# Order of the correlation, the weighted adds and the transpositions in a software-pipelined FFT-attention, mixing and LoRA-expert kernel

## What is computed

```python
# 1. LoRA of the sample's adapter, then autocorrelation attention over it
Bx = einsum('bni,bri->bnr', x, B[id]);  y = einsum('bnr,bor->bno', Bx, A[id])
corr = irfft(rfft(y) * conj(rfft(y)))             # per row, length 1024
weights, delay = top_k(corr, 6)                   # log(1024) -> 6
x = x + sum_k softmax(weights)_k * roll(y, -delay_k)
# 2. the sample's 64x64 channel mixing, then a dense layer with LoRA experts (top 2 of 8)
z = einsum('bct,bcd->bdt', x, W[id2])
x = x + z @ W_base.T + b_base + lora_experts(z)
```

## Time and profile before

| what | value |
|---|---|
| median of 3 runs | 948.55 us (946.2 to 956.33) |
| profiled execution, first to last instruction (span) | 948.1 us |
| mean granted TensorE clock, core 0 | 0.956 |
| busy: TensorE / its weight loads / VectorE / ScalarE / GpSimd | 839.0 / 705.7 / 620.8 / 336.3 / 478.5 us |

### The profile page before, as it was taken

How to read it: one execution, slowest core, us unless ns; L and a number is a source line. 1 busy time by engine, 2 the same in 40 slices (tenths; PEclk the granted TensorE clock), 3 DMA queues, 4 the chain that set the end, 5 groups by cost and what they waited for, 6 DMA issues and landing times. The chain is left out here.

```text
span 948.1 us, 16004 instructions
## 1 busy us (share of the span) xinstructions
PE 839.0 (88%) x4808; PEld 705.7 (74%) x4808; DVE 620.8 (65%) x1362; ACT 336.3 (35%) x617; POOL 478.5 (50%) x465
## 2 busy tenths in 40 slices
PE   4646899998998998998988989989989989999978
PEld 3645788777777787777877877777867778778766
DVE  2245667867677676766677576766667766777772
ACT  5343334233433333333442334333333333333311
POOL 1244544746575552755556355655337544555530
PEclk9856999999999999999999999999999989999998
DMA  8466576676766776665767667667666667777441
GB/s 277 140 195 203 185 232 213 211 239 197 232 201 203 237 240 185 212 217 184 234 202 242 192 195 214 194 208 226 193 209 194 206 212 223 234 235 234 166 146 45
DMA packets 66796, 194.48 MB, mean 205 GB/s; under 512 B 13708, under 2 KB 24236, under 8 KB 63540
## 3 DMA queue, kind: packets, MB, share of 16 engines
q0 software_dynamic: 23040, 83.90, 28.1%
q1 hardware_dynamic: 32084, 71.33, 26.8%
q10 hardware_dynamic: 11616, 38.67, 10.4%
HBM read 118.36 MB, written 50.33 MB: 178 GB/s over the span
## 5 line engine op out<-in xcount | busy, mean ns | idle before, releaser
L1093 POOL DMA_INDIRECT rolled<-y_d,off x160 | 168.6, 1054 | 297.9 <-DVE row L939 191.0
L939 DVE SCALAR_TENSOR_TENSOR row<-rolled,weight,row 128x1024 f32<-128x1024 f32 x160 | 226.5, 1416 | 101.7 <-DMA rolled<-y_d,off 98.6
L463 PE MATMUL o_ps<-wt_hi,x_hi 128*128 128x512 f32 x512 | 219.6, 429 | 0.0
L463 PE MATMUL o_ps<-wt_hi,x_lo 128*128 128x512 f32 x512 | 202.2, 395 | 0.0
L463 PE MATMUL o_ps<-wt_lo,x_hi 128*128 128x512 f32 x512 | 201.7, 394 | 0.0
L1082 POOL TENSOR_TENSOR row<-row,bias 128x1024 f32<-128x1024 f32 x32 | 77.7, 2427 | 88.1 <-PE x_ps L570 88.1
L570 PE MATMUL x_ps<-mix,row 128*128 128x128 f32 x512 | 76.5, 311 | 50.5 <-DVE row L939 32.6
L570 PEld LDWEIGHTS x_ps<-mix,row 128*128 128x128 f32 x512 | 70.4, 220 | 63.4 <-DVE row L939 38.2
L463 PEld LDWEIGHTS o_ps<-wt_hi,x_hi 128*128 128x128 f32 x512 | 96.6, 189 | 22.5 <-issue 4.8
L463 PEld LDWEIGHTS o_ps<-wt_hi,x_lo 128*128 128x128 f32 x512 | 96.2, 188 | 22.1
L463 PEld LDWEIGHTS o_ps<-wt_lo,x_hi 128*128 128x128 f32 x512 | 97.0, 189 | 14.6
(11 more groups left out here) (130 smaller groups left out, 1485.5 us busy)
## 6 DMA issues: line engine op xcount, KB each, us to landing
y_d<-y ACTq DMA_DIRECT2D x64, 512.0 KB, 3.6
row<-in_x SPq DMA_DIRECT2D x32, 512.0 KB, 7.0
adapter<-g_hi SPq DMA_DIRECT2D x64, 256.0 KB, 4.5
out<-row SPq DMA_DIRECT2D x32, 512.0 KB, 2.9
adapter<-g_lo SPq DMA_DIRECT2D x32, 256.0 KB, 4.5
r<-in_L_cond_A SPq DMA_DIRECT2D x72, 64.0 KB
r<-in_L_cond_B SPq DMA_DIRECT2D x56, 64.0 KB, 2.0
rolled<-in_L_ffn_W_base SPq DMA_DIRECT2D x5, 512.0 KB, 6.0
```

What stands on the lines that cost most here:

```text
L463: last = pe.matmul(dst, a, b, start=start and n == 0, stop=stop and n == len(todo) - 1)
L939: dve.scalar_tensor_tensor(row[u][:, :], rolled[n % RB][:, :], weight[:, n:n + 1], row[u][:, :], ALU.mult, ALU.add).then_inc(sum_step, 1)
L1093: pool.indirect_dma_start(out=rolled[n % RB][:, :], out_offset=None, in_=y2_d[u], in_offset=bass.IndirectOffsetOnAxis(ap=off[:, n:n + 1], ...
```

## The change

Three moves; no instruction is added or taken away.

1. On TensorE both halves of `x_transposed(s)` stand at the head of the slot, ahead of `project(t)`, and no longer behind the steps c = 0 and c = 1 of `base`.
2. On TensorE `correlation(s)` stands ahead of `mixed(s-1)` and no longer behind it.
3. On VectorE the low part `eo_lo` of tile s's powers stands ahead of the last weighted add (number 4) of tile s-1 and no longer behind it.

```diff
             def slot(s, u, i):
                 t, g = s - LAG, i + 1
                 attn, ffn, prep = has_attn(s), has(t), has_group(g)
+                if attn and not first(s):
+                    x_transposed(s, u, i, 0)
+                    x_transposed(s, u, i, 1)
                 if ffn:
                     project(t)
                 for c in range(KC):
                     if ffn:
                         base(t, c)
-                    if c < 2 and attn and not first(s):
-                        x_transposed(s, u, i, c)
...
                 if ffn:
                     experts(t)
+                if attn:
+                    correlation(s)
                 if has(s - 1):
...
                     mixed(s - 1, *before(u, i, 1))
-                if attn:
-                    correlation(s)
...
                 if has(last):
-                    for n in range(1, NSEL):
+                    for n in range(1, NSEL - 1):
...
                         add_rolled(last, ul, n)
                 if has_attn(s):
                     dve.wait_ge(eo_h, s + 1)
                     low(eo_lo[:, :, :].rearrange("p a r -> p (a r)"), eo[:, :, :].rearrange("p a r -> p (a r)"),
                         eo_hi[:, :, :].rearrange("p a r -> p (a r)")).then_inc(eo_l, 1)
+                if has(last):
+                    add_rolled(last, ul, NSEL - 1)
```

## The result

| | before | after |
|---|---|---|
| median | 950.45 us (4 runs, 946.2 to 956.33) | 1007.78 us (4 runs, 1006.98 to 1008.63) |
| ratio | | 1.0582, 95% interval 1.0536 to 1.0627 |
| profiled span | 948.1 us | 1006.8 us |
| mean granted TensorE clock | 0.956 | 0.921 |

The change makes the kernel 5.8% slower; predicted were 1009 us. The total is right, but several of its terms are not, as will be seen. Every ratio here is of executions in the usual state; the one of 4529.41 us that came up among ten of the kernel with move 1 alone isn't in its ratio.

What follows compares the result with a forecast made beforehand. The prediction took the chain through powers, `eo_lo`, correlation, `x_lo` and maximum, not TensorE's work, to bound the kernel. 948.1 + 52 + 8 = 1008 us of span, 1009 us as median; range 975 to 1036.

Steps and rivals of the forecast that it cites:

- What bounds the kernel: In the slot without group work, the chain of last gather, powers, `eo_lo`, correlation and maximum bounds, with the mixing hidden.
- 50 us or more: Sign in the profile after: the correlation's total wait for `eo_lo`, in nearly every slot, where 7.4 us stood.
- Correlation ahead of the mixing: At the slot's end on TensorE: mixing waits for correlation, `x_lo` ends 3.98 us after mixing starts; no early maximum.
- `eo_lo` ahead of the last add: On VectorE: the moved add, about 1.3 us, costs nothing beside the correlation; `eo` is ready 0.97 us earlier.
- 0.1 more for folds: In slots with u = 0: 0.1 us added for GpSimd's folds, within a total of +2.65 us.
- Both transpositions at the head: On TensorE at the slot's head, while the mixed tile is copied: cost 0 to 1.2 us, taken as 0.
- The 0.35 us: Per-slot gain from the earlier transposed x, bounds 0 and 0.5 us; add 0 waits for its gather and stays.
- The sum of the chain, +52 us: Slot without group work +2.2 us; six loop turns 39, slots 28 to 31 8.8, slots 1 to 3 about 4.5.
- The slots with group work: In the loop: u = 0 +2.65 us, u = 1 +0.3, u = 2 +1.1, u = 3 +2.3; a turn say 6.5.
- The clock, +8 us: Low TensorE clock behind the hole before the correlation: a third of 28 slots, 14 us, less about 6; bounds 0 and 42.
- Rival 1: Early results shorten the slot's first half more; loss about 1 us per slot, 979 us; chance 0.18.
- Rival 2: The low clock in every slot, as TensorE's hole recurs in each: 1036 us; chance 0.12.

Runs made afterwards that it cites:

- the filler: All three moves plus 14 unused transpositions on TensorE between experts and correlation, against the kernel before: 980.94 us, ratio 1.0293.
- the pieces earlier: Kernel before with move 1 and TensorE's product with B, small pieces, spectrum and adapter_out one step of base earlier: 966.18 us, ratio 1.0113.

## Why the prediction was right or wrong

- *What bounds the kernel.* Right: the powers' chain, not TensorE's work. The new wait is the one named, 68.1 us for `eo_lo` where "50 us or more" was said, and filling the waits brought nothing of the 57.9 us. Moves 2 and 3 alone each confirm that the order at the slot's end decides.
- *Correlation ahead of the mixing.* Right in mechanism: 3.88 us from the mixing's start to the end of `x_lo` (3.98 predicted), the correlation right behind `eo_lo`. The reason that I gave, that the maximum stands behind `x_lo`, is not the whole of it: with the maximum ahead of `x_lo` the kernel was slower still, because then `x_lo`, `base` and the product with B came some 3 us later.
- *`eo_lo` ahead of the last add.* Right for the moved add, which lies beside the correlation. The gain on GpSimd was 0.69 us and not 0.97, and not where I had it: the last power is short, but the one ahead of it is long. For u = 0 "0.1 more for folds" was near: the moved add was drawn out by 1.0 us, of which the mixing waits 0.24 with the filler. The rule of the Trainium skill, "SBUF — State Buffer", "Who interferes with whom", which I had cited against the change, named this place, and the trace agrees: the add of 2.29 us ends 1.08 us behind the fold that it lay beside.
- *Both transpositions at the head.* Right: 0 within the interval, alone and in company. The 0.35 us that I gave them for the slot's beginning was not theirs.
- *The sum of the chain, +52 us.* Too large. The term that failed in the plain slot is the 0.35 us for the slot's beginning, taken as bounded by the gather of add 0: the last gather ended 1.21 us sooner behind the maximum (845.93 + 1.45 against 897.16 + 1.08, 14.69 and 13.48 us). Add 0 did not stay, it began 0.76 us earlier, and the last gather was shorter by 0.37 us; what it had stood behind was the product with B. Against that the gain on the powers was 0.28 us less than predicted. Predicted were 26.4 us for that slot, measured are 25.58.
- *The slots with group work.* With the filler u = 0 and u = 3 came out 3.6 and 2.7 us longer than before, where 2.65 and 2.3 were predicted, u = 1 and u = 2 0.9 and 0.8 us shorter, where +0.3 and +1.1 were. In u = 3 the loop's end is in it. In u = 0 the slot that follows no loop's end is 1.8 us longer, the other five 3.95. What these have too much goes with the wait of 4.8 us and the product with B at half the clock behind it, which stand nowhere in my sum; no run removed them, so their share isn't shown. In u = 1 the first gather starts 2.97 us behind the maximum and no longer 5.16. In u = 2 the comparison flatters the change: four of the six slots before had the mixing at the low clock and took 30.9 to 32.3 us, the two others 29.1 and 29.6, and with the filler it is 29.9.
- *The clock, +8 us.* Too small. It was to be the net of what is there before; on the correlation and the mixing it is 35 less 13, so 22 us, and filling the hole gave 27 us back. I took a third of the slots; it fell on 22 of 31, and where it did, on the correlation, the mixing or both, up to 1.5 us each. The hole of 1.85 us that I expected was 2.14 to 2.67 in the written-out slots, for the very reason that made the chain shorter: TensorE was ahead. Here too the trace bears out the section "HAM oscillation — how this bites in real kernels" of the Trainium skill's page "TensorE: Matmul & The Clock Gate", a wait in every turn and the low clock in most of them; in move 3 alone in all.
- *Rival 1* (first half shorter, 979 us) had the mechanism of the plain slots, and its time is that of the run with the filler, 981 us. *Rival 2* was right about the clock, in part. The errors of the terms have opposite signs: 52 + 8 predicted, and of the measured 58.7 us of span some 22 are the clock on the correlation and the mixing, which leaves some 37 for the chain, the loop's end and the product with B together. So it was luck that the total came out within 2 us. That it fitted says little about the terms; only the run with the filler took them apart.
- Not predicted: at the loop's end VectorE waits for "issue" ahead of the maximum, 13.3 us in 5 ends before and 21.0 us after (up to 3.6 and 4.3 us each). It is 8 of the 58 us. The kernels with move 2 or move 3 and the search in its old place show about 4 us per end, but so does the one with the pieces earlier, which has neither (18.7 us in 5 ends). Why is open.

## What to carry to other kernels

Before an operation is put into a wait, ask what its inputs wait for: here both waited for the same late result, and the piece of work that had filled the hole was pushed out behind it. When an engine's hole comes in every turn, price its clock apart, and test with useless work in the hole; that takes one run. Two orders that each seem to remove a wait can both lose, and an edit that takes a piece out of one chain can put it into another, as the search ahead of `x_lo` did. When a total fits, check its terms one by one: here two wrong ones cancelled.

## What was not expected of the hardware

- 14 transpositions per slot that compute nothing make the kernel after 2.7% faster (1007.8 to 980.9 us), with the granted clock from 0.921 to 0.961.
- The length of the hole alone doesn't tell whether the low clock follows. In the kernel after, the holes of 1.4 to 1.7 us were followed by the full clock, those of 1.8 to 2.3 us by either: after the 2.20 us shown above the correlation ran at full speed, in the next slot, after 2.15 us (928.2 to 930.3), it took 3.2 us. With move 3 alone holes of 2.05 us and more were followed by the low clock in each of the slots 1 to 31, and in the kernel before the mixing ran at full speed behind one of 2.97 us. Slots with the same instructions so take 25.6 to 28.8 us.
- One weighted add beside GpSimd's powers holds up whichever of them it meets: the pair took 2.39 us before and 2.36 after, once with the second long and once with the first.
- The wait for "issue" at a loop's end takes different values in one program, 1.9 to 3.6 us before and 4.0 to 4.3 us after, for the same jump.
